# A graph-attention and linear-layer kernel: two s1 rows sent by DMA instead of TensorE, one row layout in pairs, earlier row sums, and a transpose between two tiles

## The chip, the cores and the metric

The kernel runs on one core of a Trainium2 chip. A core has TensorE (PE in the profile; PEld is its weight load), VectorE (DVE), ScalarE (ACT), GpSimd (POOL) and SyncE (SP), which here issues DMAs. The metric is the device time of one execution in microseconds (us), as the median of several runs. Before the change it is 379.89 us (three runs, 379.75 to 380.43).

## The reference, cut to what matters

```
def gnn(input1, input2, adj, a1, a2):          # N = M = 4096, D = 128
    e = input1 @ a1 + (input2 @ a2).T          # s1[i] + s2[j]
    e = where(e > 0, e, 0.2 * e)
    att = softmax(where(adj > 0, e, -9e15), axis=1)
    deg = sum(adj, axis=1, keepdims=True)
    att = 0.1 * (att * deg) + 0.9 * adj
    return att @ input2
x = x + gnn(layernorm(x), L0_gnn_input2, adj, L0_gnn_a1, L0_gnn_a2)
x = x + layernorm(x) @ L0_ffn_weight.T + L0_ffn_bias
```

x is [4096, 128], adj is a 4096 x 4096 matrix of zeros and ones. Since e splits into s1[i] + s2[j], the exponentials of both signs of e are products of a row factor and a column factor, and what is left per element is a test of the sign of s1[i] + s2[j].

## The kernel before, in words

The rows of x are worked in 16 chunks of 256 rows, two tiles of 128 rows each; row 2p+t of a chunk is row p of tile t. For every chunk:

- **pre_start** (VectorE) takes the moments of x and its product with a1; **row_sums** (GpSimd, L362) turns them into s1, 128 partitions by 2 tiles. **factors** (GpSimd) and **exps** (ScalarE) make the row factors.
- ScalarE needs s1 as a row of 256 on every partition, s1_bc. It comes there in one of two ways. For chunks below SPREAD (5: chunks 0 to 4) **spread** (TensorE, L635) multiplies s1 with the identity into PSUM, **copy_spread** (ScalarE, L510) copies it to s1_bc, and SP stores the row in DRAM. For the others SP stores s1 in DRAM (L295) and loads it back with a broadcast (L299). The store writes each of the 256 elements apart, since the row in DRAM is ordered by tile.
- **sign_tests** (ScalarE, L488) makes 32 tiles of steep, 8 for each of four quarters; **masks** (VectorE, L887) compares them with adj and gives plus and minus. The steep buffer holds two quarters.
- TensorE multiplies: **both** (L688) takes plus and minus of one tile, 32 matmuls of 258 columns each; **y_pair** (L702) takes adj of a chunk further on, 64 matmuls of 257 columns. y_chunk (L258) says which: chunk c+3 in the stretch of chunk c up to 11, none in 12, chunk 15 in 13, none in 14.
- **numerator** (ScalarE, L504) and **epilogue** (VectorE, L918) finish a tile. Both products of the next chunk in the same accumulators wait for it by tile_left.
- The layer norm after it: **post_start** and **post_end** (VectorE) with **post** (GpSimd, L397) between them give xn, **turn** (TensorE, L627) transposes it, **copy_turned** (ScalarE, L519) copies it out of PSUM, **linear** (TensorE, L648) multiplies it with the weights, **finish** (VectorE) adds and SP stores.

The order is written out by hand, as one instruction stream for each engine, with semaphores between them. The stretch of chunk c on an engine is called slot c. TensorE's slot c from 2 to 14 is: both for tile 0, both for tile 1, spread for chunk c+2 if it is below SPREAD, turn(c-1), y_pair if there is one, linear(c-1). ScalarE's slot c from 2 to 14 is: quarters 0 and 1 of the sign tests of chunk c+1, numerator of tile 0, quarters 2 and 3, numerator of tile 1, copies. VectorE's slot c is: linear_part (which empties the y accumulators), finish(c-2), post_end(c-1), pre_start(c+2), in slots 10 to 13 a piece of a range check, then masks of quarters 0 and 1 of chunk c+1, the epilogue of tile 0, quarters 2 and 3, the epilogue of tile 1, post_start(c). SP's turn c is: load of x for chunk c+3, store of chunk c-2's output, store and load of s1 of chunk c+2. At its end SP waits for its last stores and then takes or skips a branch to code for inputs out of range, which isn't run here.

Of the kernel before, what the change touches and what calls it, by code (L numbers as in the profile page):

```python
# [14 lines left out]
P = 128  # L15
# [23 lines left out]
GEN = 31  # L39
SPREAD = 5  # L40
AHEAD = 3


def gnn_ffn(nc, x, adj, in2, a_pair, w_t, bias, s1_rows, out):
    with ExitStack() as ctx:
# [63 lines left out]
        ac = [sb(f"ac{b}", [P, 3, TILES], F32) for b in range(2)]  # L109
        s1_bc = [sb(f"s1_bc{b}", [P, CHUNK], F32) for b in range(2)]  # L110

        num = [sb(f"num{t}", [P, WC], F32) for t in range(TILES)]
# [170 lines left out]
        def _(sp):  # L283
# [5 lines left out]
            def store_s1(n, b):  # L289
                if n < SPREAD:  # L290
                    sp.wait_ge(s1_ready, n + 1)
                    sp.dma_start(s1_rows[n:n + 1, :], s1_bc[b][0:1, :]).then_inc(s1_stored[b], 16)
                else:
                    sp.wait_ge(pre_pool, PRE * n + 3)
                    sp.dma_start(s1_rows[n].rearrange("(t p) -> p t", p=P), pre_s1[b][:, :],  # L295
                                 allow_slow_non_contiguous=True).then_inc(s1_stored[b], 16)
                    sp.wait_ge(s1_stored[b], landed(n, b))
                    sp.wait_ge(steep_done, 4 * n - 4)
                    sp.dma_start(s1_bc[b][:, :], s1_rows[n].partition_broadcast(P)).then_inc(s1_landed[b], 16)  # L299

# [11 lines left out]
            for c in range(CHUNKS):  # L312
                b = c % 2
                if c + 3 < CHUNKS:
                    load_x(c + 3, 1 - b)
                if c == 0:
                    sp.dma_start(wt_sb[:, :], w_t).then_inc(ffn_w_landed, 16)
                    sp.dma_start(bias_bc[:, :], bias.partition_broadcast(P)).then_inc(ffn_w_landed, 16)
                if c >= 2:
                    sp.wait_ge(out_ready, c - 1)  # L320
                    sp.dma_start(out[c - 2], o_buf[b]).then_inc(out_stored[b], 16)
                if c + 2 < CHUNKS:
                    store_s1(c + 2, b)
            sp.wait_ge(out_ready, CHUNKS - 1)
            sp.dma_start(out[CHUNKS - 2], o_buf[CHUNKS % 2]).then_inc(out_stored[CHUNKS % 2], 16)
            last = (CHUNKS - 1) % 2
            for t in range(TILES):
                sp.wait_ge(out_ready, CHUNKS + t)
                sp.dma_start(out[CHUNKS - 1][:, cols(t)], o_buf[last][:, cols(t)]).then_inc(out_stored[last], 16)
            count = range_left(sp)  # L330
            for b in range(2):
                sp.wait_ge(out_stored[b], 16 * CHUNKS // 2 + (16 if b == last else 0))
            for b in range(2):
                sp.wait_ge(s1_stored[b], 16 * CHUNKS // 2)
            with sp.If(count != 0):
                sp.dma_start(gen_in2[:, :, 0:D], in2.rearrange("p q j d -> p (q j) d")).then_inc(gen_weights, 16)
                with sp.Fori(0, CHUNKS) as n:
                    for q in range(QUARTERS):
                        sp.dma_start(stage[:, q, :], adj[n, q]).then_inc(gen_loaded, 16)
                    sp.dma_start(s1_bc[0][:, :], s1_rows[n].partition_broadcast(P)).then_inc(gen_loaded, 16)  # L340
                    sp.dma_start(x_in[0][:, :, :], x[n]).then_inc(gen_loaded, 16)
                    sp.wait_ge(gen_step, GEN * n + GEN)
                    sp.dma_start(out[n], o_buf[0]).then_inc(gen_stored, 16)
                    wait_apart(sp, gen_stored, 16 * n + 16)


        @block.gpsimd
        def _(pool):
# [47 lines left out]

            def post(n, b):  # L397

                wait_apart(pool, post_moments, TILES * (n + 1))
                nc.gpsimd.tensor_scalar(post_var[:, :], post_mv[:, :, 1], EPS, None,  # L400
                                        ALU.add).then_inc(post_pool, 1)
                pool.wait_ge(post_pool, 2 * n + 1)
                nc.gpsimd.tensor_tensor(post_rstd[:, :], post_var[:, :], neg_half[:, :],  # L403
                                        ALU.pow).then_inc(post_pool, 1)
                if not inner(n):
                    pool.wait_ge(ffn_w_landed, 32)
                else:
                    pool.wait_ge(out_ready, n)
                for t in range(TILES):
                    last_add = nc.gpsimd.tensor_tensor(x1_bias[:, t, :], x1[b][:, t, :], bias_bc[:, :], ALU.add)  # L410
                last_add.then_inc(x1b_ready, 1)
# [32 lines left out]
            for c in range(CHUNKS):  # L444
                b = c % 2
                if c >= 1:
                    post(c - 1, 1 - b)
                if c + 2 < CHUNKS:
                    row_sums(c + 2, b)
                if c + BUFS < CHUNKS:  # L450
                    pool.wait_ge(y_done, 2 * c + 2)
                    pool.wait_ge(minus_ready, 4 * c + 4)
                    load_adj(c + BUFS)
# [32 lines left out]
        def _(act):  # L486
            def sign_tests(n, q, b):
# [4 lines left out]
                for k in range(QJ):  # L492
                    jt = q * QJ + k
                    ins = nc.scalar.activation(steep[:, h, k, :], s1_bc[b][:, :], ACT.Relu,  # L494
                                               bias=steep_s2[:, jt:jt + 1], scale=STEEP)
# [14 lines left out]
            def copy_spread(n, b):  # L510

                act.wait_ge(s1_spread, n + 1)
                if n >= 2:
                    act.wait_ge(steep_done, 4 * n - 4)
                    act.wait_ge(plus_ready, 4 * n - 4)
                    act.wait_ge(s1_stored[b], landed(n, b) - 16)
                nc.scalar.activation(s1_bc[b][:, :], spread_ps, ACT.Copy).then_inc(s1_ready, 1)

# [62 lines left out]
            def slot(c, f):  # L581
                b = f % 2
                def prepare(q):
# [8 lines left out]
                order = [0, 1, "first", "second", 2, 3, "copies"] if c == 0 else \  # L592
                    [0, 1, "first", "second", "copies", 2, 3] if c == 1 else \
                    [0, 1, "first", 2, 3, "second", "copies"] if ahead(c, 1) else \
                    ["first", "copies", "second"]
# [30 lines left out]
        def _(pe):  # L626
# [158 lines left out]
            def slot(c, f):  # L785
# [15 lines left out]
                if c == 1:  # L801
                    for q in range(QUARTERS):
                        masked_quarter(1, q)
                    spread(3, 1)
                    pe.wait_ge(ffn_w_landed, 32)
                    turn(0)
                else:
                    for t in range(TILES):
                        pe.wait_ge(tile_left, 2 * c + t - 1)
                        both(t, b, c)  # L810
                    if c + 2 < SPREAD:
                        spread(c + 2, b)
                    turn(c - 1)
                if y_chunk(c) is not None:
# [52 lines left out]
        def _(dve):  # L867
# [231 lines left out]
            def slot(c, f):  # L1099
                b = f % 2  # L1100
                if inner(c) and y_chunk(c - 1) is not None:
                    for t in range(TILES):
# [5 lines left out]
                if not inner(c):  # L1108
# [4 lines left out]
                    masks(1, 0, 1, 1)  # L1113
                if ahead(c, 2):
                    pre_start(c + 2, b)
                if c >= RANGE_AT - QUARTERS and c < RANGE_AT:
# [49 lines left out]
            with dve.If(range_left(dve) != 0):  # L1166
                dve.wait_ge(gen_weights, 16)
                nc.vector.memset(gen_in2[:, :, D:WC], 1.0).then_inc(gen_ones, 1)
                with dve.Fori(0, CHUNKS) as n:
# [7 lines left out]
                    for jt in range(JT):  # L1177
                        k = (jt % QJ) * CHUNK
                        ins = nc.vector.tensor_scalar(gen_e[jt // QJ][:, k:k + CHUNK], s1_bc[0][:, :],
                                                      s2[:, jt:jt + 1], None, ALU.add)  # L1180
# [118 lines left out]
```

## Time and profile before

| | us |
|---|---|
| median of three runs | 379.89 |
| the profiled execution | 381.1 |
| its span, first to last instruction | 379.3 |
| TensorE busy | 362.7 |
| VectorE busy | 312.0 |
| ScalarE busy | 248.4 |
| GpSimd busy | 136.4 |

The page also says that the chain of work that ended last lies 70% on TensorE and 12% on DMA. Busy shares are averages over a start of 26 us, a steady part, and an end; the last slots differ from the steady ones, since slots 12, 14 and 15 have no adj product. The mean granted TensorE clock is 0.990.

### The profile page before, as it was taken

What the parts mean: (1) busy time and instruction counts of PE and PEld (TensorE: products, weight loads), DVE (VectorE), ACT (ScalarE), POOL (GpSimd) and SP (SyncE); (2) the same over time, 40 slices, a digit from 0 to 9 for tenths busy, and PEclk for the clock granted to TensorE, in tenths of its full rate; (3) what the DMA queues carried; (4) which work ended last, traced back from release to release, by engine and by line L of the source; (5) the groups of instructions that cost most, each with busy time, mean ns of one, the idle gap of its engine ahead of it and who ended that gap; (6) DMA issues with size and microseconds to landing.
All of it is one profiled execution on the core that took longest, in us unless ns stands there. A gap on an engine that the chain in (4) does not pass through costs nothing.

```text
span 379.3 us, 8935 instructions
## 1 busy us (share of the span) xinstructions
PE 362.7 (96%) x3231; PEld 318.1 (84%) x3231; DVE 312.0 (82%) x791; ACT 248.4 (65%) x630; POOL 136.4 (36%) x257
## 2 busy tenths in 40 slices
PE   6799999999999999999999999999999999999991
PEld 5578888888888888888888888888888887888880
DVE  5798999979999588968969787885899888999843
ACT  4599896596936494829568492944959199569210
POOL 4395723706161432507053250705125140401021
PEclk9899999999999999999999999999999999999997
DMA  7998959591926989989896998989495830010000
GB/s 245 203 214 179 218 125 189 101 185 29 212 32 44 219 49 213 20 156 104 98 164 43 214 20 174 89 110 146 54 209 15 176 78 14 16 16 15 2 29 18
DMA packets 19467, 42.06 MB, mean 111 GB/s; under 512 B 4822, under 2 KB 10716, under 8 KB 19420
## 3 DMA queue, kind: packets, MB, share of 16 engines
q0 software_dynamic: 9216, 33.56, 61.5%
q1 hardware_dynamic: 10204, 7.89, 7.4%
q8 instruction: 28, 0.46, 0.5%
q14 instruction: 19, 0.16, 0.2%
HBM read 72.88 MB, written 2.11 MB: 198 GB/s over the span
## 4 chain that ended last, share of the span: by engine, by line
PE 70%; DMA 12%; ACT 5%; issue 5%; DVE 5%; POOL 2%; DVEq 0%; POOLq 0%
PE acc_y L675 21%; PE acc_v L696 18%; PE acc_u L693 18%; DMA s_rows<-pre_s 6%; ACT steep L494 5%; DMA s_bc<-s_rows 4%; PE acc_v L675 4%; PE acc_u L675 3%; DMA adj_all<-adj 2%; PE small L658 1%; PE acc_u L664 1%; DVE plus L892 1%; PE acc_v L664 1%; PE turned L632 1%; PE turned L675 0%
## 5 line engine op out<-in xcount | busy, mean ns | idle before, releaser
L494 ACT ACTIVATE steep<-s_bc,steep_s 128x256 bf16<-128x256 f32 x512 | 208.0, 496 | 81.2 <-DMA s_bc<-s_rows 71.8
L696 PE MATMUL acc_v<-weights_v,minus 128*128 128x258 f16 x864 | 191.0, 272 | 0.0
L693 PE MATMUL acc_u<-weights_u,plus 128*128 128x258 f16 x864 | 191.0, 273 | 0.0
L675 PE MATMUL acc_y<-weights_y,adj_all 128*128 128x257 f16 x960 | 108.5, 273 | 0.0
L675 PEld LDWEIGHTS acc_y<-weights_y,adj_all 128*128 128x128 bf16 x960 | 93.1, 97 | 12.5
L693 PEld LDWEIGHTS acc_u<-weights_u,plus 128*128 128x128 bf16 x864 | 83.6, 97 | 11.6
L696 PEld LDWEIGHTS acc_v<-weights_v,minus 128*128 128x128 bf16 x864 | 84.0, 97 | 11.0
L892 DVE TENSOR_TENSOR plus<-adj_all,steep 128x2048 bf16<-128x2048 bf16 x64 | 78.5, 1226 | 15.8 <-ACT steep L494 15.6
L895 DVE TENSOR_TENSOR minus<-adj_all,plus 128x2048 bf16<-128x2048 bf16 x64 | 78.4, 1225 | 2.2
L400 POOL TENSOR_SCALAR post_var<-post_mv 128x2 f32<-128x2 f32 x15 | 3.2, 213 | 160.9 <-DVE post_mv L957 160.9
L358 POOL DMA_DIRECT2D adj_all<-adj x64 | 36.0, 581 | 6.6 <-DMA plus<-in 4.6
L507 ACT ACTIVATE num<-acc_u,ac 128x129 f32<-128x129 f32 x32 | 11.4, 364 | 25.0 <-PE acc_u L693 19.7
L908 DVE SCALAR_TENSOR_TENSOR lin<-acc_y,x_in 128x128 f32<-128x128 f32 x30 | 8.6, 285 | 14.7 <-issue 14.5
L410 POOL TENSOR_TENSOR late<-x,bias_bc 128x128 f32<-128x128 f32 x30 | 13.4, 464 | 19.9 <-DVE late L978 19.9
L675 PE MATMUL acc_v<-weights_v,minus 128*128 128x258 f16 x128 | 15.4, 273 | 0.0
L931 DVE SCALAR_TENSOR_TENSOR num<-acc_v,ac,num 128x129 f32<-128x129 f32 x32 | 11.3, 353 | 4.1 <-PE acc_v L664 3.0
L675 PE MATMUL acc_u<-weights_u,plus 128*128 128x258 f16 x112 | 13.5, 272 | 0.5 <-POOL weights_u L429 0.5
L675 PEld LDWEIGHTS acc_v<-weights_v,minus 128*128 128x128 bf16 x128 | 12.4, 97 | 1.7
L965 DVE TENSOR_SCALAR late<-x,post_mv,post_rstd 128x128 f32<-128x128 f32 x30 | 11.5, 424 | 1.9 <-POOL post_rstd L403 1.8
L389 POOL TENSOR_SCALAR ac_arg<-pre_h 128x2 f32<-128x2 f32 x16 | 11.8, 735 | 3.0 <-POOL pre_h L385 3.0
L385 POOL TENSOR_SCALAR pre_h<-pre_s,g_col 128x2 f32<-128x2 f32 x16 | 12.6, 787 | 0.8 <-POOL pre_s L377 0.6
L675 PEld LDWEIGHTS acc_u<-weights_u,plus 128*128 128x128 bf16 x112 | 10.8, 97 | 2.2 <-issue 0.8
(116 smaller groups left out, 334.0 us busy)
## 6 DMA issues: line engine op xcount, KB each, us to landing
adj_all<-adj POOLq DMA_DIRECT2D x64, 512.0 KB, 14.6
x_in<-x SPq DMA_DIRECT2D x16, 128.0 KB, 9.2
plus<-in SPq DMA_DIRECT2D x4, 512.0 KB, 5.7
out<-late SPq DMA_DIRECT2D x15, 128.0 KB, 3.6
s_bc<-s_rows SPq DMA_DIRECT2D x11, 128.0 KB, 8.7
s_rows<-pre_s SPq DMA_DIRECT2D x11, 1.0 KB
out<-late SPq DMA_DIRECT2D x2, 64.0 KB, 2.5
s_rows<-s_bc SPq DMA_DIRECT2D x5, 1.0 KB
```

What stands on the lines that cost most here:

```text
L358: nc.gpsimd.dma_start(adj_b[n % BUFS][:, q * QJ:(q + 1) * QJ, :].rearrange("p a b -> p (a b)"), adj[n, q]).then_inc(adj_landed[n % BUFS][q ...
L385: nc.gpsimd.tensor_scalar(pre_h[:, :], pre_s1[b][:, :], g_col[:, 0:1], None, ALU.add).then_inc(pre_pool, 1)
L389: nc.gpsimd.tensor_scalar(ac_arg[b][:, 0, :], pre_h[:, :], 1.0 - SLOPE, 0.0, ALU.mult, ALU.min).then_inc(pre_pool, 1)
L410: last_add = nc.gpsimd.tensor_tensor(x1_bias[:, t, :], x1[b][:, t, :], bias_bc[:, :], ALU.add)
L494: ins = nc.scalar.activation(steep[:, h, k, :], s1_bc[b][:, :], ACT.Relu, bias=steep_s2[:, jt:jt + 1], scale=STEEP)
L507: nc.scalar.activation(num[t][:, :], acc_u[t][:, 0:WC], ACT.Copy, scale=ac[b][:, 0, t:t + 1]).then_inc(num_ready, 1)
L675: ends[t] = nc.tensor.matmul(acc[t][:, 0:width], left[:, jt, cols(t)], right[:, jt, :, :].rearrange("p a b -> p (a b)")[:, 0:width], start ...
L693: last_u = nc.tensor.matmul(acc_u[t][:, 0:2 * WC], plus[b][:, jt, cols(t)], w_u[:, jt, :, :].rearrange("p a b -> p (a b)"), start=(jt == 0 ...
L696: last_v = nc.tensor.matmul(acc_v[t][:, 0:2 * WC], minus[b][:, jt, cols(t)], w_v[:, jt, :, :].rearrange("p a b -> p (a b)"), start=(jt == ...
L892: nc.vector.tensor_tensor(plus[b][:, qs, :], adj_b[f][:, qs, :], steep[:, q % 2, :, :], ALU.is_gt).then_inc(plus_ready, 1)
L895: nc.vector.tensor_tensor(minus[b][:, qs, :], adj_b[f][:, qs, :], plus[b][:, qs, :], ALU.subtract).then_inc(minus_ready, 1)
L965: ins = nc.vector.tensor_scalar(xn[:, t, :], x1[b][:, t, :], post_mv[:, t, 0:1], post_rstd[:, t:t + 1], ALU.subtract, ALU.mult)
```

## The change: what it does

- SPREAD goes from 5 to 3. The s1 rows of chunks 3 and 4 go by DRAM, as those of 5 to 15 did.
- The row is kept in pairs everywhere: element 2p+t is row p of tile t. The store writes 128 runs of two elements. ScalarE reads s1_bc with a step of two elements (s1_tiles) and writes steep in the old order; copy_spread writes s1_bc with that step.
- SP's store and load of s1 are parted: the store stands first in turn c, then the x load and the output store, then the load. 
- VectorE's pre_start(c+2) stands first in the slot. GpSimd's post is parted into post_factor and post_bias, with row_sums between them.
- In slots 12 and 14, which have no y_pair, TensorE's turn(c-1) stands between the two tiles, and ScalarE's copies stand right after the numerator of tile 0.
- SP takes its branch first and then waits for the last stores.

```
-SPREAD = 5
+SPREAD = 3
@@ tiles
+        s1_tiles = [s[:, :].rearrange("q (p t) -> q t p", t=TILES) for s in s1_bc]
@@ SP, store_s1, else:
-                    sp.dma_start(s1_rows[n].rearrange("(t p) -> p t", p=P), pre_s1[b][:, :],
-                                 allow_slow_non_contiguous=True).then_inc(s1_stored[b], 16)
-                    sp.wait_ge(s1_stored[b], landed(n, b))
-                    sp.wait_ge(steep_done, 4 * n - 4)
-                    sp.dma_start(s1_bc[b][:, :], s1_rows[n].partition_broadcast(P)).then_inc(s1_landed[b], 16)
+                    sp.dma_start(s1_rows[n].rearrange("(p t) -> p t", t=TILES), pre_s1[b][:, :]).then_inc(s1_stored[b], 16)
+            def load_s1(n, b):
+                sp.wait_ge(s1_stored[b], landed(n, b))
+                sp.wait_ge(steep_done, 4 * n - 4)
+                sp.dma_start(s1_bc[b][:, :], s1_rows[n].partition_broadcast(P)).then_inc(s1_landed[b], 16)
@@ SP, for c in range(CHUNKS)
+                if c + 2 < CHUNKS and c + 2 >= SPREAD:
+                    store_s1(c + 2, b)
                 if c + 3 < CHUNKS:
                     load_x(c + 3, 1 - b)
...
                 if c + 2 < CHUNKS:
-                    store_s1(c + 2, b)
+                    if c + 2 < SPREAD:
+                        store_s1(c + 2, b)
+                    else:
+                        load_s1(c + 2, b)
@@ SP, the end
-            count = range_left(sp)
-            for b in range(2):
-                sp.wait_ge(out_stored[b], 16 * CHUNKS // 2 + (16 if b == last else 0))
-            for b in range(2):
-                sp.wait_ge(s1_stored[b], 16 * CHUNKS // 2)
-            with sp.If(count != 0):
+            with sp.If(range_left(sp) != 0):
+                stores_done()
...
+            stores_done()
@@ GpSimd
                 if c >= 1:
-                    post(c - 1, 1 - b)
+                    post_factor(c - 1)
                 if c + 2 < CHUNKS:
                     row_sums(c + 2, b)
+                if c >= 1:
+                    post_bias(c - 1, 1 - b)
@@ ScalarE
-                    ins = nc.scalar.activation(steep[:, h, k, :], s1_bc[b][:, :], ACT.Relu,
+                    ins = nc.scalar.activation(steep[:, h, k, :].rearrange("q (t p) -> q t p", t=TILES), s1_tiles[b],
+                                               ACT.Relu,
                                                bias=steep_s2[:, jt:jt + 1], scale=STEEP)
...
-                nc.scalar.activation(s1_bc[b][:, :], spread_ps, ACT.Copy).then_inc(s1_ready, 1)
+                nc.scalar.activation(s1_tiles[b], spread_ps.rearrange("q (t p) -> q t p", t=TILES), ACT.Copy).then_inc(s1_ready, 1)
...
+                    [0, 1, "first", "copies", 2, 3, "second"] if ahead(c, 1) and y_chunk(c) is None else \
                     [0, 1, "first", 2, 3, "second", "copies"] if ahead(c, 1) else \
@@ TensorE
-                    spread(3, 1)
...
-                    for t in range(TILES):
-                        pe.wait_ge(tile_left, 2 * c + t - 1)
-                        both(t, b, c)
+                    pe.wait_ge(tile_left, 2 * c - 1)
+                    both(0, b, c)
+                    if y_chunk(c) is None:
+                        turn(c - 1)
+                    pe.wait_ge(tile_left, 2 * c)
+                    both(1, b, c)
                     if c + 2 < SPREAD:
                         spread(c + 2, b)
-                    turn(c - 1)
+                    if y_chunk(c) is not None:
+                        turn(c - 1)
@@ VectorE, slot(c, f)
+                if inner(c) and ahead(c, 2):
+                    pre_start(c + 2, b)
...
-                if ahead(c, 2):
-                    pre_start(c + 2, b)
+                if not inner(c):
+                    pre_start(2, 0)
```

The first place is TensorE at the end of slot 12. Before, the transposes of xn into turned (L632) and the two products of linear (L658) follow each other directly behind the last of both's matmuls (L693, L696):

```order
L693 MATMUL acc_u<-weights_u,plus 128x258
L696 MATMUL acc_v<-weights_v,minus 128x258
L632 MATMUL turned<-ident,late 128x128 x2
L658 MATMUL small<-wt_sb,late 128x128 x2
L693 MATMUL acc_u<-weights_u,plus 128x258
L696 MATMUL acc_v<-weights_v,minus 128x258
```

After, in the middle of slot 12 (first two rows: the end of tile 0; L649 is turn) and at its end (L675 is linear):

```order
L710 MATMUL acc_u<-weights_u,plus 128x258
L713 MATMUL acc_v<-weights_v,minus 128x258
L649 MATMUL turned<-ident,late 128x128 x2
L710 MATMUL acc_u<-weights_u,plus 128x258
L713 MATMUL acc_v<-weights_v,minus 128x258
...
L710 MATMUL acc_u<-weights_u,plus 128x258
L713 MATMUL acc_v<-weights_v,minus 128x258
L675 MATMUL small<-wt_sb,late 128x128 x2
L710 MATMUL acc_u<-weights_u,plus 128x258
```

The 64 matmuls of tile 1 now stand between turn and linear. The second place is VectorE at the start of slot 12: before, linear_part (L908 to L914), finish (L978), post_end (L965), then pre_start (L874 and on):

```order
L911 TENSOR_SCALAR deg_0<-acc_y 128x1
L914 SCALAR_TENSOR_TENSOR lin_2_0<-acc_y,lin_2_0 128x128
L908 SCALAR_TENSOR_TENSOR lin_2_1<-acc_y,x_in 128x128
L911 TENSOR_SCALAR deg_1<-acc_y 128x1
L914 SCALAR_TENSOR_TENSOR lin_2_1<-acc_y,lin_2_1 128x128
L978 TENSOR_TENSOR late<-small,late 128x256
L965 TENSOR_SCALAR late<-x_1,post_mv,post_rstd 128x128 x2
L874 BN_STATS pre_st<-x_in 128x6 x2
```

After, with pre_start (L894 to L902) ahead of linear_part (L928 and on):

```order
L977 BN_AGGR post_mv<-post_st 128x2 x2
L894 BN_STATS pre_st<-x_in 128x6 x2
L897 BN_AGGR pre_mv<-pre_st 128x2 x2
L902 SCALAR_TENSOR_TENSOR pre_prod,pre_dot<-x_in,pre_mv,a_bc 128x128 x2
L928 SCALAR_TENSOR_TENSOR lin_2_0<-acc_y,x_in 128x128
L931 TENSOR_SCALAR deg_0<-acc_y 128x1
```

Six instructions moved from behind post_end to the front; their number is the same. The third place is SP's queue in turns 1 and 2, before (s_rows is the row in DRAM, s_bc the broadcast tile, L292 the store behind copy_spread):

```order
L292 DMA s_rows<-s_bc 1x256
L287 DMA x_in<-x 128x256
L292 DMA s_rows<-s_bc 1x256
L287 DMA x_in<-x 128x256
L321 DMA out<-late 128x256
L292 DMA s_rows<-s_bc 1x256
```

and after, where L296 stores chunks 3 and 4 and L301 loads them:

```order
L293 DMA s_rows<-s_bc 1x256
L296 DMA s_rows<-pre_s_1 128x2
L288 DMA x_in<-x 128x256
L301 DMA s_bc<-s_rows 128x256
L296 DMA s_rows<-pre_s_0 128x2
L288 DMA x_in<-x 128x256
L325 DMA out<-late 128x256
L301 DMA s_bc<-s_rows 128x256
```

The store of s1 is now ahead of the x load and the output store, and the load of s1 behind them.

## Rows read from the trace of the kernel before

**Rows 1.** The page, part 1: busy us, share of the span, instructions.
```profile
PE 362.7 (96%) x3231; PEld 318.1 (84%) x3231; DVE 312.0 (82%) x791; ACT 248.4 (65%) x630; POOL 136.4 (36%) x257
```
**Rows 2.** Waits: who waited for whom, us in total, times, longest.
```profile
PE small L658 <- ACT late L523: 1.2, 2, 0.8
...
SPq L299 <- DMA s_rows<-pre_s: 94.9, 11, 12.5
```
**Rows 3.** Windows: stretch, its us, busy us of each engine, clock, DMA share, GB/s.
```profile
82.75:105.00 22.25, 22.25 (x205) 19.72 (x203) 21.02 (x52) 19.01 (x51) 7.21 (x15) 1.00 0.58 118
...
301.26:317.03 15.77, 15.02 (x136) 13.10 (x134) 14.17 (x33) 13.75 (x36) 5.00 (x9) 1.00 0.40 87
317.03:338.84 21.81, 21.81 (x201) 19.27 (x198) 19.84 (x49) 13.97 (x36) 4.88 (x11) 1.00 0.10 14
338.84:354.34 15.50, 15.03 (x137) 13.11 (x135) 14.70 (x35) 14.06 (x36) 1.82 (x4) 1.00 0.03 10
```
**Rows 4.** The chain that ended last: start us, us, what; slots 1, 2, 13.
```profile
74.75 0.45 PE small L644 x4
...
97.00 0.45 PE small L644 x4
...
331.51 7.05 PE acc_y L675 x64
```
**Rows 5.** Timeline, end of slot 12: start us, us, instruction, [idle before <-releaser].
```profile
316.06 0.37 ACT L523 ACTIVATE late<-turned 128x256 f32<-128x256 f32 x1
...
316.49 0.71 PE L658 MATMUL small<-wt_sb,late 128*128 128x128 f32 x4 [0.75 <-ACT late L523]
```
**Rows 6.** Timeline, slot 15, VectorE, TensorE and ScalarE at turn(14).
```profile
358.83 0.25 DVE L957 BATCH_NORM_AGGREGATE post_mv<-post_st 128x2 f32<-128x6 f32 x2
...
360.32 0.88 DVE L965 TENSOR_SCALAR late<-x,post_mv,post_rstd 128x128 f32<-128x128 f32 x2 [0.90 <-POOL post_rstd L403]
361.28 0.25 PEld L632 LDWEIGHTS turned<-ident,late 128*128 128x128 f32 x2
...
361.80 0.38 ACT L523 ACTIVATE late<-turned 128x256 f32<-128x256 f32 x1
```
**Rows 7.** Timeline, VectorE, slots 12 to 14.
```profile
300.97 0.29 DVE L908 SCALAR_TENSOR_TENSOR lin<-acc_y,x_in 128x128 f32<-128x128 f32 x1 [1.10 <-issue]
...
316.40 1.22 DVE L892 TENSOR_TENSOR plus<-adj_all,steep 128x2048 bf16<-128x2048 bf16 x1
...
321.36 0.25 DVE L957 BATCH_NORM_AGGREGATE post_mv<-post_st 128x2 f32<-128x6 f32 x2
...
322.84 0.88 DVE L965 TENSOR_SCALAR late<-x,post_mv,post_rstd 128x128 f32<-128x128 f32 x2 [0.89 <-POOL post_rstd L403]
...
341.75 0.25 DVE L957 BATCH_NORM_AGGREGATE post_mv<-post_st 128x2 f32<-128x6 f32 x2
...
343.44 0.74 DVE L965 TENSOR_SCALAR late<-x,post_mv,post_rstd 128x128 f32<-128x128 f32 x2
```
**Rows 8.** Timeline, slot 1, VectorE and GpSimd.
```profile
66.62 0.26 DVE L908 SCALAR_TENSOR_TENSOR lin<-acc_y,x_in 128x128 f32<-128x128 f32 x1
...
68.77 0.47 DVE L874 BATCH_NORM_STATS2 pre_st<-x_in 128x6 f32<-128x128 f32 x2
...
70.92 0.54 POOL L377 TENSOR_TENSOR pre_s<-pre_dot,pre_rstd 128x2 f32<-128x2 f32 x1
```
**Rows 9.** Line L299, the s1 load, all eleven: issue to landing.
```profile
DMA to landing us min/median/max: 3.4/8.7/9.7
```
**Rows 10.** Groups by form: xcount | busy us, mean ns | idle before.
```profile
L494 ACT ACTIVATE steep<-s_bc,steep_s 128x256 bf16<-128x256 f32 x512 | 208.0, 496 | 81.2 <-DMA s_bc<-s_rows 71.8 <-DVE plus L892 9.3
...
L542 ACT ACTIVATE weights_v<-minus 128x1024 f16<-128x1024 f32 x4 | 4.2, 1049 | 0.1
```
**Rows 11.** Lines L335 and L45, the end: duration ns, first and last start us.
```profile
L335 SPq COMPARE_BRANCH  x1: 50/50/50, 377.9 to 377.9; - x1
...
L45 POOLq DRAIN  x1: 5304/5304/5304, 373.7 to 373.7; - x1
```

More of the change, by code:

```diff
@@ L329, in _, with stores_done @@
                 sp.dma_start(out[CHUNKS - 1][:, cols(t)], o_buf[last][:, cols(t)]).then_inc(out_stored[last], 16)
-            count = range_left(sp)
-            for b in range(2):
-                sp.wait_ge(out_stored[b], 16 * CHUNKS // 2 + (16 if b == last else 0))
-            for b in range(2):
-                sp.wait_ge(s1_stored[b], 16 * CHUNKS // 2)
-            with sp.If(count != 0):
+            def stores_done():
+                for b in range(2):
+                    sp.wait_ge(out_stored[b], 16 * CHUNKS // 2 + (16 if b == last else 0))
+                for b in range(2):
+                    sp.wait_ge(s1_stored[b], 16 * CHUNKS // 2)
+            with sp.If(range_left(sp) != 0):
+                stores_done()
                 sp.dma_start(gen_in2[:, :, 0:D], in2.rearrange("p q j d -> p (q j) d")).then_inc(gen_weights, 16)
@@ L395, in factors, with post_factor @@
                                         ALU.add).then_inc(pre_pool, 1)
-            def post(n, b):
+            def post_factor(n):
                 wait_apart(pool, post_moments, TILES * (n + 1))
@@ L404, in post, with post_bias @@
                                         ALU.pow).then_inc(post_pool, 1)
+            def post_bias(n, b):
                 if not inner(n):
@@ L1178, in _ @@
                         k = (jt % QJ) * CHUNK
-                        ins = nc.vector.tensor_scalar(gen_e[jt // QJ][:, k:k + CHUNK], s1_bc[0][:, :],
+                        ins = nc.vector.tensor_scalar(gen_e[jt // QJ][:, k:k + CHUNK].rearrange("q (t p) -> q t p", t=TILES),
+                                                      s1_tiles[0],
                                                       s2[:, jt:jt + 1], None, ALU.add)
```

## The prediction, made before the result was known

> **What bounds the kernel now.** The page's busy times come first: TensorE 96%, VectorE 82%, ScalarE 65% [rows 1]. So only what TensorE executes or waits for can move the end, unless another engine is brought up to it. The waits of TensorE come next: from 27 us to 368 us it waits twice, both times linear's product for ScalarE's copy of the transposed xn, 1.2 us in all [rows 2]. The windows then say what the two waits cost, with weight loads that have lost their overlap: slot 13 takes 21.81 us, of which y_pair is 7.05 [rows 4], so a slot without y_pair should take 14.76. Slot 12 takes 15.77 and slot 14 takes 15.50 [rows 3]: 1.01 and 0.74 us are lost. The last view is the timeline at the ends of these slots. In slot 12 the copy starts at 316.06 and the product at 316.49 [rows 5]; the copy stands behind eight sign tests and a numerator. Behind TensorE, VectorE is nearly as late: in slot 15 xn of chunk 14 is finished at 361.20 and the transpose loads its weights at 361.28 [rows 6], 0.08 us of slack.
>
> **Spreads of chunks 3 and 4.** They are two pieces of four passes, 0.45 us each in the chain [rows 4]; slot 2, which has one, takes 22.25 against 21.81 [rows 3], so 0.44. Nothing lies over them. Gain 0.45 + 0.44 = 0.89 us. The two copies on ScalarE go too.
>
> **Turn between the tiles.** In slots 12 and 14 transposes and products stay the same in number. The copy now has tile 1's 64 matmuls, 7.05 us, for a wait of 0.4 us. Gain 1.01 + 0.74 = 1.75 us. This holds if xn is there a tile earlier. For turn(11) that is at 301.26 - 0.89 + 7.05 = 307.4, and VectorE starts linear_part at 300.97; from there to the end of post_end it takes 344.18 - 342.00 = 2.2 us, as slot 14 shows [rows 7], so xn is ready by 303.2. For turn(13): TensorE's slot 14 starts at 338.84 - 0.89 - 1.01 = 336.94, turn at 344.0. At VectorE's old pace its post_start ends at 342.00 [rows 7], and post_end 2.2 later, at 344.2: by that alone 0.2 us would be lost.
>
> **Row sums first.** What VectorE executes is the same. Its waits change. At the start of slot 12 it waits 1.10 us for y_pair's end, and in slot 13 0.89 us for GpSimd's post_rstd [rows 7]; pre_start now lies over both. So VectorE gains where it is late. Slot 12 first: the copy can start 361.80 - 354.34 = 7.46 after the slot's start [rows 3, 6], that is at 307.83, then 16 sign tests at 208.0/512 = 0.406 us [rows 10] end at 307.83 + 0.3 + 6.5 = 314.6. The mask of the last quarter then starts at 314.65 instead of 316.40, and post_start ends 5.21 later [rows 7], at 319.86, 1.75 earlier. Slot 13 took 342.00 - 321.61 = 20.39 us with 0.89 idle [rows 7]; without it the end is at 339.36, 2.64 earlier. Slot 14 has no idle on VectorE, so slot 15's xn is ready at 361.20 - 2.64 = 358.56, and TensorE, 0.89 + 1.75 earlier, asks for it at 358.64. Both streams move by 2.64 and the slack stays 0.08. I cost this edit at nothing, but the 1.75 above needs it.
>
> **s1 of chunks 3 and 4 by DMA.** In slot 1 the row sums ended 71.46 - 68.77 = 2.69 after pre_start's start; pre_start moves to 66.62 [rows 8], so the store goes out at 69.4. Store to load took 94.9/11 = 8.6 us at most 12.5 [rows 2], the load 8.7, at most 9.7 [rows 9]. s1_bc of chunk 3 is there at 86.7, at worst 91.6. Needed: TensorE starts slot 3 at 105.00 - 0.45 = 104.55 and its last quarter 48 x 0.110 = 5.3 later (0.110 is 7.05/64). Sign tests 32 x 0.406 = 13.0, a numerator 0.4, an epilogue and the mask pairs behind give some 16.8 in all, so s1 may come until 93. It costs 0. Queued behind the store's wait on SP is the x load of chunk 4, first used a slot of 21.8 us later, and in a load of the same size the longest landing is 9.7 [rows 9]. Chunk 4's row is out by 90 and needed 21 us later than chunk 3's; also 0. The row sums' early start lets the later rows arrive earlier too, and ScalarE's waits for them shrink; no TensorE wait hangs on them.
>
> **The row in pairs.** The store has half as many runs. Bounds for it: nothing changes (8.6 us), or it halves to 4.3; I take no change, since either is off the path. ScalarE's read with a step of 8 bytes is nowhere in the trace. Below: 0. Above: the rate per element halves. The nearest row is a plain 1024-element activation, 1.05 us [rows 10], 1.02 ns an element, so up to 256 x 1.02 = 0.26 us for each sign test. I take 0, the nearest row's rate, and keep the upper end as a rival.
>
> By the Trainium skill, "SBUF — State Buffer" (section "Door 1: The DMA port swizzle"), accesses that stay at two or more in a line of 16 bytes run at full rate; a step of 8 bytes is just two. By it the cost is 0; no run here shows it yet.
>
> **SP's branch.** It takes 0.05 us and stands at 377.9. GpSimd's DRAIN ends at 373.7 + 5.3 = 379.0 [rows 11] and SP is not the last. Gain 0; at most 0.2.
>
> **Sum.** 0.89 + 1.75 = 2.64 us. The profiled execution takes 381.1, so one like it would take 378.5; the median of three, 1.2 below it, becomes 379.89 - 2.64 = 377.25. I say 377.3.
>
> **Rivals.**
>
> *A VectorE wait takes the place of the stalls.* TensorE comes 2.64 us earlier to turn(14), and VectorE has to follow within 0.08. For it: slack is that thin, and the estimate of 319.86 rests on ScalarE and VectorE both being ready within 0.1 to 0.3 us. Against: pre_start over two idle spots is sure. If VectorE only keeps the 0.89 of the spreads, the end comes 0.89 + 0.08 = 0.97 earlier: 378.9. Halfway: 378.1.
>
> *Only the spreads count, or not even they.* The two stalls of slots 12 and 14 come back elsewhere in full, and s1 of chunk 3 comes late besides. The first alone gives 379.89 - 0.89 = 379.0; if the row comes at 94, 1 us past the limit, 0.9 of it is gone and there is no change, 379.9. For: the row now takes a DMA store and load in place of a matmul. Against: 91.6 takes both worst waits already.
>
> *Slower: the strided read.* ScalarE reads s1_bc with the step in all 512 sign tests. From some 0.05 us each it decides: 16 in slot 12 and 16 in slot 14 stand between turn and the last mask, 24 in the start, 56 x 0.047 = 2.64. At the upper end of 0.26, 32 of them add 8.3 to 14.06 busy in slot 14 [rows 3], 22.4 a slot, over 21.81: 0.6 in each of 12 long slots (7), 22.4 - 14.76 = 7.6 in slots 12 and 14 (15), 24 x 0.26 = 6 in the start: 28 us, 405. Against: nothing in the rows makes a step costly; for: no row has one.
>
> *The change doesn't deliver early rows*: on SP the load of s1 now stands behind the output store, which waits for finish. Then ScalarE waits as before; TensorE waits for none of it and still ends earlier, by 2.64 or by what the first rival leaves: 377.3 to 378.
>
> **Chances.** Forecast 0.64, the VectorE wait 0.19, only the spreads or less 0.09 (0.02 of it at 379.0 or below), strided read 0.06, late rows 0.02. About 0.2% (0.8 us) is what a measurement of this kernel tells from no change. Faster by more: 0.64 + 0.19 + 0.02 + 0.02 = 0.87. Within: the other 0.07 of the second rival. Slower: 0.06. The range goes from 376.7 (SP's 0.2 and 0.3 of spread between runs below the forecast) to 378.8, which takes in nearly all of the VectorE wait.
>
> **What would show it.** Right: slot 2 at 21.81; slots 12 and 14 at 14.8; no wait of small for ScalarE; the stretch of the 8.6 us between store and load at 4 to 9; idle of ScalarE before sign tests well under 71.8. ScalarE's interval between two sign tests 0.40, as now; at 0.45 or more the strided read is what happened. A wait of turned for VectorE in slot 14 or 15 is the first rival, and its length is what is missing from 2.64. A wait of acc_u or acc_v in slot 3 for masks means that chunk 3's row came too late. If TensorE has no new waits and the time still isn't 2.6 less, the prediction is wrong in its sum.

## The result, and the profile after

| us | before | after |
|---|---|---|
| median, range (6 runs each) | 380.68 (379.75 to 381.48) | 377.95 (377.61 to 379.05) |
| the profiled execution, its span | 381.1, 379.3 | 378.14, 376.3 |
| first u matmul of chunk 0 | 26.11 | 25.45 |

The ratio is 0.9936, with a 95% interval of 0.9914 to 0.9959: 0.6% faster. Ratios here and below leave out executions that took over 1.5% longer than the fastest of the same kernel. The prediction said 377.3, in a range of 376.7 to 378.8.

The two spans differ by 3.0 us, of which 0.66 lies ahead of the first u matmul of chunk 0. That start is no part of the change: in the ten other traces of this study it lies between 24.56 and 27.39. So from here on stretches are counted from that matmul, and "the stream" is the time from it to the last transposes, turn(14); behind these the kernel takes 17.9 us both times. The stream was 335.28 us and is 332.88, 2.40 less.

The busy times, to set beside [rows 1]:

```profile
PE 360.9 (96%) x3223; PEld 317.2 (84%) x3223; DVE 314.4 (84%) x791; ACT 256.6 (68%) x628; POOL 139.4 (37%) x257
```

TensorE has 8 instructions less, the two spreads. ScalarE has 2 fewer, and still 8 us more of busy time. The windows of slots 1, 2, 12, 13 and 14, to set beside [rows 3]:

```profile
59.82:81.64 21.82, 21.82 (x200) 19.28 (x198) 18.76 (x39) 18.63 (x47) 8.16 (x16) 1.00 0.86 159
81.64:103.45 21.81, 21.81 (x201) 19.27 (x198) 20.72 (x48) 14.44 (x36) 8.04 (x15) 1.00 0.63 117
299.71:314.47 14.76, 14.76 (x137) 13.07 (x134) 12.41 (x25) 7.62 (x20) 3.03 (x8) 1.00 0.15 28
314.47:336.27 21.80, 21.80 (x200) 19.27 (x198) 20.68 (x51) 18.24 (x46) 4.87 (x11) 1.00 0.11 13
336.27:351.04 14.77, 14.77 (x137) 13.08 (x135) 13.70 (x33) 10.74 (x28) 1.82 (x4) 1.00 0.03 11
```

From start to start the slots took 22.28, 22.25, 15.78, 21.81 and 15.50 us before, and 21.83, 21.80, 14.76, 21.80 and 14.76 now: 0.45 + 0.45 + 1.02 + 0.74 = 2.66, and TensorE has no gap between its matmuls from the first of them to slot 15. The waits of linear for ScalarE, 1.2 us of [rows 2], are gone. But the stream got only 2.40. The rest is at its end, in slot 15. The timeline of VectorE and TensorE there, to set beside [rows 6]:

```profile
355.91 0.25 DVE L977 BATCH_NORM_AGGREGATE post_mv<-post_st 128x2 f32<-128x6 f32 x2
...
357.39 0.89 DVE L985 TENSOR_SCALAR late<-x,post_mv,post_rstd 128x128 f32<-128x128 f32 x2 [0.90 <-POOL post_rstd L413]
...
357.98 0.27 PE L713 MATMUL acc_v<-weights_v,minus 128*128 128x258 f16 x1
358.33 0.44 PE L649 MATMUL turned<-ident,late 128*128 128x128 f32 x2
```

xn of chunk 14 ends at 358.28, and turn(14) starts 0.35 us behind the start of the matmul before it. Where it waits for nothing it follows at 0.11 (experiment 1), so about 0.24 us is lost; 2.66 - 2.40 gives 0.26. That is the first rival of the prediction, in a small dose.

ScalarE's groups, the sign tests first, to set beside [rows 10], and SP's waits, to set beside [rows 2]:

```profile
L509 ACT ACTIVATE steep<-s_bc,steep_s 128x256 bf16<-128x256 f32 x512 | 217.9, 518 | 16.5 <-DVE plus L912 8.6 <-DMA s_bc<-s_rows 7.9
```

```profile
SPq L301 <- DMA s_rows<-pre_s: 26.1, 13, 3.0
```

Each sign test went from 496 to 518 ns. They overlap, so the interval between two starts is the better measure: its median went from 0.399 to 0.419 us. ScalarE's waits for the row fell from 71.8 to 7.9 us. And from the issue of the s1 store to that of the load behind it there were 9.1 us in the mean before (7.6 to 13.0; SP's wait alone is the 8.6 of the prediction), and 3.6 now (2.7 to 4.9), although SP now issues the x load and the output store in between. SP's timeline in turns 1 and 2 shows the rows of chunks 3 and 4:

```profile
68.62 0.35 SPq L296 DMA_DIRECT2D s_rows<-pre_s  x1
69.07 0.38 SPq L288 DMA_DIRECT2D x_in<-x  x1
72.21 0.34 SPq L301 DMA_DIRECT2D s_bc<-s_rows  x1
89.25 0.34 SPq L296 DMA_DIRECT2D s_rows<-pre_s  x1
89.69 1.52 SPq L288 DMA_DIRECT2D x_in<-x  x1
91.26 0.43 SPq L325 DMA_DIRECT2D out<-late  x1
91.94 0.33 SPq L301 DMA_DIRECT2D s_bc<-s_rows  x1
```

The two loads landed at 81.45 and 104.23.

### The profile page after: what moved, and what is told of

Its sections match the earlier page's. It is cut to its first block, busy times and chain, and to the rows that moved or that the text cites. A ratio compares the mean times of both kernels' runs of the same rounds, so it can differ in the third digit from the quotient of the medians.

```text
span 376.3 us, 8915 instructions
## 1 busy us (share of the span) xinstructions
PE 360.9 (96%) x3223; PEld 317.2 (84%) x3223; DVE 314.4 (84%) x791; ACT 256.6 (68%) x628; POOL 139.4 (37%) x257
## 4 chain that ended last, share of the span: by engine, by line
PE 88%; DMA 3%; issue 2%; DVE 2%; ACT 2%; POOL 2%; DVEq 0%; POOLq 0%
PE acc_y L692 28%; PE acc_u L710 23%; PE acc_v L713 23%; PE acc_v L692 4%; DMA adj_all<-adj 3%; PE acc_u L692 3%; PE small L675 2%; ACT steep L509 2%; PE acc_u L681 1%; PE acc_v L681 1%; PE turned L649 1%; POOL adj_all L368 1%; DVE plus L912 0%; POOL pre_s L387 0%; DVE late L985 0%
## 5 line engine op out<-in xcount | busy, mean ns | idle before, releaser
L509 ACT ACTIVATE steep<-s_bc,steep_s 128x256 bf16<-128x256 f32 x512 | 217.9, 518 | 16.5 <-DVE plus L912 8.6
L912 DVE TENSOR_TENSOR plus<-adj_all,steep 128x2048 bf16<-128x2048 bf16 x64 | 80.5, 1259 | 19.3 <-ACT steep L509 19.3
L710 PEld LDWEIGHTS acc_u<-weights_u,plus 128*128 128x128 bf16 x864 | 83.6, 97 | 11.5
L523 ACT ACTIVATE num<-acc_u,ac 128x129 f32<-128x129 f32 x32 | 11.4, 363 | 79.9 <-PE acc_u L710 75.0
L395 POOL TENSOR_SCALAR pre_h<-pre_s,g_col 128x2 f32<-128x2 f32 x16 | 22.4, 1402 | 0.3 <-POOL pre_s L387 0.2
L951 DVE SCALAR_TENSOR_TENSOR num<-acc_v,ac,num 128x129 f32<-128x129 f32 x32 | 11.3, 353 | 4.1 <-PE acc_v L681 3.0
L399 POOL TENSOR_SCALAR ac_arg<-pre_h 128x2 f32<-128x2 f32 x16 | 13.6, 847 | 3.0 <-POOL pre_h L395 3.0
L946 DVE SCALAR_TENSOR_TENSOR num<-acc_u,ac,num 128x129 f32<-128x129 f32 x32 | 11.1, 348 | 2.7 <-ACT num L523 2.7
L928 DVE SCALAR_TENSOR_TENSOR lin<-acc_y,x_in 128x128 f32<-128x128 f32 x30 | 8.5, 285 | 5.1 <-issue 4.7
L955 DVE SCALAR_TENSOR_TENSOR num<-acc_v,ac,num 128x129 f32<-128x129 f32 x32 | 11.3, 353 | 1.1
## 6 DMA issues: line engine op xcount, KB each, us to landing
adj_all<-adj POOLq DMA_DIRECT2D x64, 512.0 KB, 11.2
```

Of the source, the lines that this page charges most:

```text
L395: nc.gpsimd.tensor_scalar(pre_h[:, :], pre_s1[b][:, :], g_col[:, 0:1], None, ALU.add).then_inc(pre_pool, 1)
L399: nc.gpsimd.tensor_scalar(ac_arg[b][:, 0, :], pre_h[:, :], 1.0 - SLOPE, 0.0, ALU.mult, ALU.min).then_inc(pre_pool, 1)
L509: ins = nc.scalar.activation(steep[:, h, k, :].rearrange("q (t p) -> q t p", t=TILES), s1_tiles[b], ACT.Relu, bias=steep_s2[:, jt:jt + 1], ...
L523: nc.scalar.activation(num[t][:, :], acc_u[t][:, 0:WC], ACT.Copy, scale=ac[b][:, 0, t:t + 1]).then_inc(num_ready, 1)
L710: last_u = nc.tensor.matmul(acc_u[t][:, 0:2 * WC], plus[b][:, jt, cols(t)], w_u[:, jt, :, :].rearrange("p a b -> p (a b)"), start=(jt == 0 ...
L912: nc.vector.tensor_tensor(plus[b][:, qs, :], adj_b[f][:, qs, :], steep[:, q % 2, :, :], ALU.is_gt).then_inc(plus_ready, 1)
```

## The experiments

Two questions stood: how the 2.40 us divides over the edits, and why turn(14) waits. The theory for the second was that ScalarE's read with a step costs 0.02 us a sign test, and that the sign tests between the copy and the last mask make VectorE 0.3 us late. "Stream" is as above. Ratios are to runs of the kernel before on the same chip.

**1. The row by tile again.** All of the change, but the store scatters 256 elements of 4 bytes into a row ordered by tile, as before, and ScalarE reads without a step.

```
-        s1_tiles = [s[:, :].rearrange("q (p t) -> q t p", t=TILES) for s in s1_bc]
+        s1_tiles = [s[:, :].rearrange("q (t p) -> q t p", t=TILES) for s in s1_bc]
-                    sp.dma_start(s1_rows[n].rearrange("(p t) -> p t", t=TILES), pre_s1[b][:, :])
+                    sp.dma_start(s1_rows[n].rearrange("(t p) -> p t", p=P), pre_s1[b][:, :], ...)
```

> The changed kernel with the s1 row back in the order by tile: the store writes 256 runs of 4 bytes, ScalarE and copy_spread go over s1_bc with unit step (as two rows of 128). Everything else as changed. Theory: the step of 8 bytes is what took ScalarE's interval between sign tests from 0.399 to 0.419 us, and 32 of them on the path to the last masks are the 0.3 us for which turn(14) waits in slot 15. So interval 0.399, no wait at turn(14), 2.9 us faster than before, and the wait from store to load back at 8.6 us (7.6 to 9.2) on SP. Rival a: it is the two-row form of the operand, not the step: interval stays 0.419 and the time stays 2.6 faster. Rival b: the store got short because it now goes out ahead of the adj loads: then store to load stays at 3.5 us here too.

378.34 us (377.00 to 379.17), ratio 0.9919 (0.9889 to 0.9950). The interval is 0.399 us, the stream 332.63, 0.25 less than with pairs, and turn(14) doesn't wait. Its groups of ScalarE, SP's waits and TensorE's timeline at turn(14):

```profile
L510 ACT ACTIVATE steep<-s_bc,steep_s 128x256 bf16<-128x256 f32 x512 | 207.9, 495 | 58.1 <-DMA s_bc<-s_rows 51.0 <-DVE plus L913 6.9
```

```profile
SPq L302 <- DMA s_rows<-pre_s: 97.0, 13, 9.1
```

```profile
359.32 0.27 PE L714 MATMUL acc_v<-weights_v,minus 128*128 128x258 f16 x1
359.43 0.38 PE L650 MATMUL turned<-ident,late 128*128 128x128 f32 x2
```

Counted from the first u matmul, VectorE's last post_mv of chunk 12 ends at 293.80 by tile and at 294.11 in pairs; those of chunks 13 and 14 are 0.33 apart. In slot 12 that is 16 x 0.02: VectorE's last plus, the mask of the last quarter, waits for the 16 sign tests behind the copy. But it isn't simply carried on to the end, for in slot 14 VectorE waits for ScalarE once more, 0.30 us in both kernels. The 16 sign tests behind the copy and the last plus of slot 14, first by tile, then in pairs:

```profile
345.37 6.48 ACT L510 ACTIVATE steep<-s_bc,steep_s 128x256 bf16<-128x256 f32 x16
351.95 1.23 DVE L913 TENSOR_TENSOR plus<-adj_all,steep 128x2048 bf16<-128x2048 bf16 x1 [0.30 <-ACT steep L510]
```

```profile
344.02 6.82 ACT L509 ACTIVATE steep<-s_bc,steep_s 128x256 bf16<-128x256 f32 x16
350.94 1.22 DVE L912 TENSOR_TENSOR plus<-adj_all,steep 128x2048 bf16<-128x2048 bf16 x1 [0.30 <-ACT steep L509]
```

The first of the 16 starts 318.57 us after the first u matmul in both kernels, the last ends 0.34 us later in pairs. So by these rows what turn(14) waits for is set by slot 14's own 16 tests, and the 0.31 of slot 12 alone would be taken up by VectorE's wait of 0.30 there. The expectation counted 32 tests for 0.3 us, where 32 x 0.02 would be 0.6; the two sixteens don't add. The long way through DRAM is back with the old store, 97.0/13 = 7.5 us of wait, and costs nothing.

**2. The spreads alone.** The kernel before, with chunks 3 and 4 by DMA.

```
-SPREAD = 5
+SPREAD = 3
@@ TensorE
-                    spread(3, 1)
```

> The kernel before with only SPREAD 5 to 3 (rows of chunks 3 and 4 by DMA, no spread of chunk 3). Theory: 0.89 us faster, slots 1 and 2 at 21.8 instead of 22.28 and 22.25, slots 12 and 14 still at 15.8 and 15.5, no wait for masks in slot 3. Rival: the row of chunk 3 comes late here (stored at 71.4, 8.6 + 8.7 later, 88.7; limit 93): a wait in slot 3 takes back part.

380.71 us, ratio 1.0012 (0.9987 to 1.0037): no gain in the medians, though the stream is 334.50, 0.78 less. A gain of 0.78 would be a ratio of 0.998, just outside this interval; its one trace has the latest first u matmul of all, 27.39, and why the medians don't show the gain stays open. Slot 1 is 21.83, slot 2 22.19, with a wait that isn't there in the changed kernel. The row of chunk 3 landed 64.0 us after the first u matmul, against 56.0 there, and ScalarE's copy for linear(1) stands behind its sign tests:

```profile
104.81 0.37 ACT L523 ACTIVATE late<-turned 128x256 f32<-128x256 f32 x1
105.23 0.52 PEld L658 LDWEIGHTS small<-wt_sb,late 128*128 128x128 f32 x4 [0.41 <-ACT late L523]
```

So the spreads' second 0.45 needs an early row. In experiment 1, where the row landed at 61.7, linear(1) didn't wait; in the trace of experiment 10 it landed at 64.0 again, and slot 2 took 22.19 again. Of the 0.78, 0.28 is slot 12, which took 15.50 here because its copy was less late; the spreads themselves gave 0.51. The waits of [rows 2] have none of this kind in slot 2, and the prediction asked only whether the masks would be in time, up to 93.

**3. Turn between the tiles alone.** The kernel before, with this edit on TensorE and ScalarE.

```
+                    if y_chunk(c) is None:
+                        turn(c - 1)
...
@@ ScalarE
+                    [0, 1, "first", "copies", 2, 3, "second"] if ahead(c, 1) and y_chunk(c) is None else \
```

> The kernel before with only the turn between the tiles in slots 12 and 14 and ScalarE's copies moved with it. Theory: slots 12 and 14 at 14.76 (1.75 us less), but VectorE, with its idle 0.89 us in slot 13 uncovered, moves only 0.85 earlier, so turn(14) in slot 15 waits for xn by about 0.8 us: 0.9 us faster in all. Rival: the stalls alone count, and it is 1.75 faster, with no wait at turn(14).

380.35 us, ratio 0.9993 (0.9960 to 1.0025), stream 334.41. Slots 12 and 14 are 14.76 each, 1.76 us less, and 0.9 of it comes back in slot 15, where VectorE is now behind:

```profile
359.88 0.88 DVE L970 TENSOR_SCALAR late<-x,post_mv,post_rstd 128x128 f32<-128x128 f32 x2 [0.90 <-POOL post_rstd L403]
360.81 0.20 PEld L633 LDWEIGHTS turned<-ident,late 128*128 128x128 f32 x2 [1.01 <-DVE late L970]
```

**4. Row sums late again.** The changed kernel, with pre_start behind post_end and GpSimd's post in one piece.

```
-                if inner(c) and ahead(c, 2):
-                    pre_start(c + 2, b)
@@ behind post_end
+                if ahead(c, 2):
+                    pre_start(c + 2, b)
...
```

> The changed kernel with pre_start back behind post_end on VectorE and post undivided ahead of row_sums on GpSimd. Theory: VectorE's idle spots are open again, the wait at turn(14) grows from 0.3 by 0.9 to about 1.2 us: 1.4 to 1.8 us faster than before in place of 2.6. Also the rows of s1 come some 4 to 5 us later, ScalarE waits for them again, no wait on TensorE from that. Rival: row sums first gives nothing to the time: 2.6 faster, wait at turn(14) still 0.3.

379.73 us, ratio 0.9969 (0.9946 to 0.9991), stream 333.78: 0.9 more than the changed kernel. All slots up to 14 are as short as there; the wait at turn(14) is longer than in any other kernel:

```profile
359.55 0.88 DVE L984 TENSOR_SCALAR late<-x,post_mv,post_rstd 128x128 f32<-128x128 f32 x2 [0.90 <-POOL post_rstd L413]
360.48 0.20 PEld L648 LDWEIGHTS turned<-ident,late 128*128 128x128 f32 x2 [1.26 <-DVE late L984]
```

From store to load it took 2.8 to 4.9 us here too, though the store goes out as late as before; so the short way is the store's own. The loads landed 11.5 us after issue in the median, against 8.5.

**5 and 6. Both orders of the row once more**, the changed kernel and the one of the first experiment, on one chip, twelve executions each.

> The changed kernel itself, once more beside the kernel before and the next one. From the first u matmul of chunk 0 to turn(14) it should take 332.9 us as in its first profile (before: 335.3), with the wait of 0.3 us at turn(14); in the median 2.4 us faster than before, and 0.2 to 0.3 slower than the kernel with the row by tile. Where the start (up to that first matmul) lies between 25.4 and 27.4 us, that moves the single time by as much and tells nothing of the change.

> The changed kernel with the s1 row by tile, as in e1, beside the changed kernel. Theory: no wait at turn(14), 332.6 us from the first u matmul to it, some 0.3 us faster than the changed kernel and 2.7 faster than before. Rival: SP's 9 us from store to load, in place of 3.5, costs something in the median that the profile did not show, and it is the slower of the two.

In pairs 378.40 us, ratio 0.9954 (0.9926 to 0.9981); by tile 378.49, ratio 0.9931 (0.9907 to 0.9955). The median by tile is over all twelve executions; two of them, without a trace, took 386.0 and 388.0 us and are left out of the ratio. In pairs the longest of twelve took 381.5. The streams repeat to 0.01 us, 332.89 and 332.63, the intervals too, 0.419 and 0.400. The 0.25 us is sure in the traces and too small for the medians: the intervals overlap, and which of the two is faster isn't settled by them.

**7 and 10. Two rows with a unit step.** By tile as in experiment 1, but with a gap of 8 elements between the tiles' rows of s1_bc, so that ScalarE's operand has two rows without a step. The seventh run is one execution, the tenth eleven executions of the same kernel.

```
-        s1_bc = [sb(f"s1_bc{b}", [P, CHUNK], F32) for b in range(2)]
+        s1_bc = [sb(f"s1_bc{b}", [P, TILES, P + 8], F32) for b in range(2)]
+        s1_tiles = [s[:, :, 0:P] for s in s1_bc]
...
```

> As e1, but s1_bc has a gap of 8 elements between its two rows of 128, so that ScalarE's operand is two rows with unit step and can't be merged into one row of 256, as it was in e1. Theory (the step costs): interval between two sign tests 0.399. Rival (the two-row form costs): 0.419, as in the changed kernel, and a wait at turn(14) again.

> The same kernel as the one with the two tiles' rows apart by a gap and read by unit steps, which took 390.09 us in its one look because the load of chunk 4's row landed 22.2 us after its issue. Theory: that landing was an accident of one execution (the loads of all other chunks land in 10 to 12 us there, of which TensorE has room for every one), so the median is that of row by tile, 378.3 to 378.8, ratio 0.992 to 0.995, and TensorE waits nowhere between the first u matmul and the last transposes. Rival: the load in runs of half a row is late at chunk 4 in every execution, because it meets the same adj loads each time; then the median is again near 388 to 390, slower than before by 2%, with a wait of linear for ScalarE's copy in slot 3 and half a clock behind it.

What was asked is answered: the interval is 0.399 us, so two rows are free and the step is what costs. What wasn't foreseen is the time, 390.09 us. The wait, slots 3 and 4, and the load of the row:

```profile
PE small L676 <- ACT late L540: 8.7, 1, 8.7
```

```profile
104.33:135.53 31.20, 22.53 (x200) 19.68 (x198) 17.61 (x44) 14.81 (x39) 6.11 (x15) 0.90 0.75 129
135.53:159.34 23.81, 23.81 (x199) 20.31 (x198) 22.26 (x62) 12.88 (x34) 8.99 (x18) 0.91 0.62 71
```

```profile
DMA to landing us min/median/max: 3.5/11.2/22.2
```

The row of chunk 4 landed 22.2 us after its issue at 98.47, the sign tests came late, ScalarE's copy for linear(2) behind them, and linear waited 8.7 us. TensorE stood from 125.8 to 134.5. In the middle of that, at 129.4, the granted clock fell from 2.4 to 1.2 GHz, and it stayed there for 10.2 us. The two halves of this stretch (the columns are those of [rows 3]):

```profile
129.38:134.52 5.14, 0.00 (x1) 0.00 (x1) 4.86 (x12) 5.14 (x16) 0.00 (x0) 0.50 0.56 112
134.52:139.61 5.09, 5.09 (x23) 3.81 (x24) 4.67 (x13) 5.09 (x14) 0.00 (x0) 0.50 0.00 0
```

In the second half, 5.1 us, matmuls followed each other at 0.215 us instead of 0.110. So 8.7 us of wait became 31.20 + 23.81 - 2 x 21.81 = 11.4 us of time: the wait, and 2.7 us for 5.1 us of work at the lower clock.

The repetition bears out neither the expectation of an accident nor the rival of a late row in every execution. The median is 378.98, the ratio 0.9978 (0.9942 to 1.0015), but the eleven executions lie apart: five at 377.9 to 378.2, five from 379.0 to 382.8, and one at 391.4, which the ratio leaves out. The profiled one is that last one, and has the same load late again. ScalarE's wait for it:

```profile
121.88 6.49 ACT L510 ACTIVATE steep<-s_bc,steep_s 128x256 bf16<-128x256 f32 x16 [18.60 <-DMA s_bc<-s_rows]
```

Issued at 98.46, landed at 121.85. On its way it meets the four adj loads issued from 90.28 on. The busy tenths of the 16 DMA engines from 96 to 123 us, in slices of 0.675 us:

```profile
DMA  6311424999999999999998431590029605262983
```

They are full from 101 to 110, but the row lands 11 us behind that, in a stretch with little traffic, so the adj loads alone don't explain it. The row isn't late alone: the last of the four adj loads lands beside it, at 122.01, and in experiment 7 at 120.55, with the row at 120.70; in experiment 1 that adj load landed at 116.5 and the row at 107.3. In the changed kernel the load of chunk 4 goes out at 91.94 and takes 12.3 us, the longest of its thirteen. Why it takes 22 us in some executions, whether the load in runs of half a row is needed for it, and whether the other long executions, the two by tile of experiment 6 among them, have this cause, stays open: they have no trace.

**8. Half the store.** The changed kernel, where from chunk 3 on only tile 0's 128 elements of 4 bytes are stored and loaded; tile 1's half of the row isn't brought.

```
-                    sp.dma_start(s1_rows[n].rearrange("(p t) -> p t", t=TILES), pre_s1[b][:, :])
+                    sp.dma_start(s1_rows[n, 0:P].rearrange("(p t) -> p t", t=1), pre_s1[b][:, 0:1], ...)
```

> The changed kernel, but only tile 0's half of s1 is stored (128 runs of 4 bytes, side by side in DRAM) and loaded from chunk 3 on; tile 1's half of s1_bc keeps old values, so that part of the computation is left out. If the number of runs sets the wait from store to load: 3.5 us, as for 128 runs of 8 bytes. If the size of a run does (4 bytes against 8): near 8.6. If both, some 4 to 5 us (128 of the 256 short runs). Time as the changed kernel within 0.3.

378.81 us in one execution. SP's waits:

```profile
SPq L302 <- DMA s_rows<-pre_s: 84.1, 13, 8.5
```

With the same number of runs as in pairs, 128, and half their size, store to load is back at 7.2 to 9.8 us, 8.1 in the mean; with 256 such runs it was 9.3 (experiment 1), with 128 of 8 bytes 3.6. So it is mainly their size of 4 bytes that makes the old store slow, and their number adds little.

**9. SP's branch behind its waits again**, else as changed.

```
-            with sp.If(range_left(sp) != 0):
-                stores_done()
+            count = range_left(sp)
+            stores_done()
+            with sp.If(count != 0):
...
-            stores_done()
```

> The changed kernel with one edit undone: SyncE again waits for its last stores first and only then takes or skips its branch. My theory: SyncE is not the last engine, GpSimd's DRAIN and TensorE's end outlast it, and the branch itself takes 0.05 us, so the time is the changed kernel's 378.0 to 378.4 within 0.2 us, and the stretch from the first u matmul to the last transpose stays 332.88. Rival: the end of the program hangs on SyncE's branch, then up to 0.2 us more, 378.2 to 378.6, and SyncE's branch would be the last instruction of the span.

378.09 us, ratio 0.9937 (0.9909 to 0.9966). From the first u matmul to the last instruction both take 350.82 us. The end in this kernel, SP's branch and GpSimd's DRAIN, to set beside [rows 11]:

```profile
L345 SPq COMPARE_BRANCH  x1: 50/50/50, 376.2 to 376.2; - x1
```

```profile
L45 POOLq DRAIN  x1: 5304/5304/5304, 372.2 to 372.2; - x1
```

The DRAIN ends at 377.5, 1.3 us behind the branch. The edit is worth nothing.

## Why the prediction was right, and where it was off

**Spreads: right.** 0.89 us was forecast, 0.45 + 0.45 came. Experiment 2 shows the condition that the prediction didn't see: with the row of chunk 3 eight us later, the copy for linear(1) is late and 0.39 of it stays in slot 2. From the first u matmul on, 61.7 was early enough and 64.0 was not. The prediction's worst case of 91.6, which it called free, is 65.5 on this scale, and its limit of 93 is 66.9; both are too late for this copy. The forecast landing of 86.7 is 60.6, and the row came at 56.0, since the store to load time wasn't 8.6 but 3.6.

**Turn between the tiles: right.** 1.01 + 0.74 were forecast, 1.02 + 0.74 came, and experiment 3 has them alone. It also shows what the edit is worth by itself, 0.87 us of the stream.

**Row sums first: right that it costs nothing and that the 1.75 needs it.** Undoing it lost 0.9 us, all at turn(14). The three edits aren't a sum: the spreads alone give 0.78 and the turn alone 0.87, together with the row sums 2.65 (by tile). Neither of the first two can be told from nothing in the medians. The row sums first were not run alone, so that they cost and give nothing by themselves is argued, not shown.

**The slack of 0.08 us: the step that was off, by 0.3 us.** The prediction put xn of chunk 14 at 358.56 in the trace of before, that is 332.45 after the first u matmul. By tile it came at 359.29 - 26.80 = 332.49, and nothing waited. In pairs it came at 358.28 - 25.45 = 332.83, 0.34 later. That agreement to 0.04 us is in part luck. By tile against before, VectorE gained 1.69 us up to the end of slot 12 (forecast 1.75), 1.30 in slot 13 (forecast 0.89), and lost 0.38 in slot 14 (forecast 0), where it waits 0.30 us for ScalarE, whose copy now stands ahead of the last 16 sign tests. "Slot 14 has no idle on VectorE" held for the trace of before and not for the changed kernel, and the two errors cancel. What made turn(14) wait is the price of the strided read, taken as 0. It is 0.020 us a sign test; the bounds were 0 and 0.26. The rival's count of the tests, 16 + 16 + 24, was too high besides: of slots 12 and 14 only one sixteen reaches the end, and the 24 of the start can't be seen beside its scatter. Of the 0.34, 0.24 went to the end.

The rule of the Trainium skill, "SBUF — State Buffer" (section "Door 1: The DMA port swizzle"), that two or more accesses in a line of 16 bytes run at full rate, as a step of 8 bytes would, isn't what the traces show: 0.399 us without the step, 0.419 with it, and experiment 7 puts it on the step and not on the two rows. The measurement decides: 5% on ScalarE's read of float32.

**The row in pairs.** It was to be free either way, and it isn't: the store takes 5 us less, which TensorE never sees in the traces, and the sign tests 10 us more of ScalarE's time (217.9 against 207.9), of which the end sees 0.25. In the stream it loses; in the medians the two orders can't be told apart.

**SP's branch: right,** 0.

**The sum** was 2.64 and the stream gave 2.40; the medians gave 380.68 - 377.95 = 2.7, with the start's scatter of up to 2.8 us between traces in each of them. The forecast of 377.3 took the median of three runs, 379.89, as its base; from the 380.68 of six runs it would have been 378.04, against 377.95. That the medians come so near to 2.64 is luck, as the stream gave 0.24 less.

## What to carry to other kernels

Where several stalls lie behind each other on a path, an edit's worth alone tells little: two edits that gave 0.78 and 0.87 us of the stream alone, and nothing in the median, gave 2.65 with the third (by tile), which gives the late engine its slack. Ask of each edit who is late next, and of an early row how late it may come for every reader behind it in the queue, copies too, not only for its own masks. And price an access pattern by one run before it stands in 512 instructions.

## What was not expected of the hardware

- ScalarE reads float32 with a step of 8 bytes 5% slower than without it, 0.419 against 0.399 us for 128 x 256.
- A store of single 4-byte elements to DRAM was 7.5 to 13.6 us from its issue to that of the load behind it for 256 runs, with one of 15.8 (experiment 2), and 7.2 to 9.8 us for 128; one of 128 runs of 8 bytes 2.7 to 4.9 us.
- A broadcast load of 128 KB that lands in 11.2 us in the median of its kernel (in runs of half a row; 8.5 in runs of a whole row) took 22.2 and 23.4 us in two executions, at the same place, with adj loads of 512 KB each under way.
- In a wait of TensorE of 8.7 us the granted clock fell to 1.2 GHz, for 10.2 us, of which 5.1 lay behind the wait; it cost 11.4 us in all.
